# Grouped attention's front: a search round spread over gaps, keys and queries in a new order

## The reference

```python
# layer 1, feed-forward
xq = int4_quant(x); gate = square(relu(xq @ w_gate_q)); up = xq @ w_up_q      # 512 -> 1376
x = x + int8_quant(up * gate) @ w_down_q                                       # 1376 -> 512
# layer 2, grouped attention: 32 query heads of 128, 8 key/value heads, context of 512
q = rmsnorm(layernorm(x) @ q_proj); k = rmsnorm(ctx @ k_proj); v = ctx @ v_proj
x = x + softmax(q @ k.T * scale + mask) @ v @ o_proj
# layer 3, attention: which of the 512 context rows are among the 154 largest, feature by feature
_, topk_idx = top_k(moveaxis(channel_map, 1, 2), 154)
```

## Time and profile before

| | us |
|---|---|
| median of three runs (lowest, highest) | 877.66 (877.02, 878.44) |
| the profiled execution's own time | 877.61 |
| its span, first to last instruction | 875.9 |
| TensorE busy in the span | 782.7 (89%) |
| VectorE busy | 716.4 (82%) |
| ScalarE busy | 519.3 (59%) |
| GpSimd busy | 429.3 (49%) |

### The profile page before, as it was taken

One profiled execution on the slowest core, in us unless ns is written; L12 is line 12 of the kernel. 1 busy time (PEld: TensorE's weight loads), 2 busy tenths in 40 slices (PEclk: granted clock), 3 DMA queues, 4 the chain that ended last, 5 costly groups with the idle time before them and its releaser, 6 DMA issues. The chain is left out here.

```text
span 875.9 us, 16423 instructions
## 1 busy us (share of the span) xinstructions
PE 782.7 (89%) x5140; PEld 635.4 (73%) x5146; DVE 716.4 (82%) x1732; ACT 519.3 (59%) x1408; POOL 429.3 (49%) x380
## 2 busy tenths in 40 slices
PE   1976899858978999999999999999999999678878
PEld 0474676524767898898898898898898898565456
DVE  7878998958777887887887887887887887964975
ACT  6864898846347557557557557557557557321421
POOL 3237087805225845845845845845845845622110
PEclk9999999979979999999999999999999999789989
DMA  8253245562300310310310310310310320203001
GB/s 309 87 176 138 75 146 198 172 195 76 91 7 1 118 53 8 108 53 5 108 55 6 101 61 2 104 62 1 100 66 0 101 67 0 72 25 117 1 0 49
DMA packets 39114, 68.23 MB, mean 78 GB/s; under 512 B 5729, under 2 KB 18593, under 8 KB 38946
## 3 DMA queue, kind: packets, MB, share of 16 engines
q1 hardware_dynamic: 39074, 67.73, 23.6%
HBM read 62.38 MB, written 5.34 MB: 77 GB/s over the span
## 5 line engine op out<-in xcount | busy, mean ns | idle before, releaser
L2230 DVE TENSOR_SCALAR_CACHE_REDUCE xn<-ctxT,candidate 128x512 bf16<-128x512 f32 x248 | 174.4, 741 | 0.1
L1962 ACT ACTIVATE layer_attention_probs<-xnT,stats 128x512 f32<-128x512 f32 x128 | 93.9, 734 | 133.7 <-DVE stats L2070 133.7
L1746 PE MATMUL bank<-layer_attention_keysT,layer_attention_queriesT 128*128 128x512 f32 x384 | 124.9, 435 | 3.3 <-DVE layer_attention_queriesT L2063 3.3
L2082 DVE TENSOR_TENSOR layer_attention_probsT<-bank,layer_attention_probsT 128x512 fp32r<-128x512 f32 x128 | 88.1, 688 | 40.7 <-ACT layer_attention_probsT L1970 39.4
L1746 PEld LDWEIGHTS bank<-layer_attention_probsT,layer_attention_values 128*128 128x128 f32 x768 | 99.9, 191 | 19.2 <-issue 9.1
L1746 PE MATMUL bank<-layer_attention_probsT,layer_attention_values 128*128 128x256 f32 x768 | 103.5, 285 | 10.2 <-DVE layer_attention_probsT L2082 9.9
L1970 ACT CAST layer_attention_probsT<-bank 128x512 fp32r<-128x512 f32 x128 | 74.8, 584 | 52.0 <-PE bank L1821 52.0
L1746 PE MATMUL bank<-layer_attention_wo,layer_attention_headsT 128*128 128x512 f32 x384 | 102.2, 409 | 3.8 <-issue 3.0
L1693 POOL TENSOR_TENSOR layer_attention_mixed<-layer_attention_mixed,xnT 128x512 f32<-128x512 f32 x32 | 52.2, 1632 | 86.8 <-DMA xnT<-inverse_sums 85.4
L1746 PE MATMUL bank<-layer_attention_l_wq,layer_attention_xnT 128*128 128x512 f32 x384 | 93.6, 392 | 0.7 <-DVE layer_attention_xnT L2131 0.7
L1746 PEld LDWEIGHTS bank<-layer_attention_l_wkv,layer_context_parts 128*128 128x128 f32 x720 | 88.4, 188 | 2.8
(11 more groups left out here) (320 smaller groups left out, 1664.2 us busy)
## 6 DMA issues: line engine op xcount, KB each, us to landing
layer_attention_l_raw_qo<-in_wqT SPq DMA_DIRECT2D x9, 1024.0 KB, 5.1
xnT<-inverse_sums SPq DMA_DIRECT2D x16, 512.0 KB, 3.7
layer_attention_l_raw_qo<-in_woT SPq DMA_DIRECT2D x8, 1024.0 KB, 6.8
tw_raw<-in_w_gateT SPq DMA_DIRECT2D x8, 688.0 KB, 5.4
tw_raw<-in_w_upT SPq DMA_DIRECT2D x8, 688.0 KB, 4.2
tw_raw<-in_w_downT SPq DMA_DIRECT2D x6, 768.0 KB, 4.5
layer_attention_l_raw_kv<-in_wkvT SPq DMA_DIRECT2D x9, 512.0 KB, 4.9
ternary<-tw_rounded SPq DMA_DIRECT2D x8, 344.0 KB, 2.7
```

What stands on the lines that cost most here:

```text
L1746: last = pe.matmul(out, stationary[f][a], moving[f][b], start=f == 0 and x == 0, stop=f == count - 1 and x == 2)
L1962: a.activation(probs[:, u % 3, :], masked[:, u % 2, :], ACT.Exp, bias=negmax[:, u:u + 1], scale=-1.0, accum_out=sums[:, u:u + 1]).then_inc ...
L2082: v.tensor_tensor(probsT[:, 1, p % 2, :, columns], T[u % 2][:, :].rearrange("p (c q) -> p c q", c=CPB), probsT[:, 0, p % 2, :, columns], A ...
L2230: own(k.nc.vector.tensor_scalar(k.flags[:, r % 2], row_tile(k.ctxT, r), k.candidate[:, r:r + 1].bitcast(F32), 0.0, ALU.is_gt, ALU.add, acc ...
```

## The change

Three things are done.

1. The search round that stood as one block in the front is taken apart. Its first two counts go into the feed-forward, ahead of and behind the first `inner_chunk`. Counts three and four stay in the front, behind the keys' low part. The update comes behind the last low part of the queries. These four counts write their flags into the first row of `k.xnT`, which nothing else uses then; the maximum of unit 0 writes there next and now waits for them.
2. TensorE projects both query tiles of the first batch before it turns tiles 2 and 3 of x. The keys are turned between the halves of the second tile's projection. The scores of unit 0 are made before the turn of query tile 1.
3. VectorE makes the low part of x's tile 0 before the last update, and the norm of tile 3 is spread out. ScalarE copies query tile 0, turns out the keys, then copies query tile 1. GpSimd scales the keys before the last root of x's norm.

The same counts, products and copies are made as before; their places, the scratch tile of four counts and the waits that go with them are what differs.

```diff
@@ feed-forward, VectorE
+                bisection_count(k, own, 0, first_flags(k))
                 for c in range(NC):
                     inner_chunk(0, c)
+                    if c == 0:
+                        bisection_count(k, own, 1, first_flags(k))
@@ front, GpSimd
-                for t in range(TPB, TILES):
-                    tile_norm_gpsimd(k, n, t)
 ...
-                for c in TURNS:
-                    norm(start, own, c)
+                tile_norm_gpsimd(k, n, 2)
+                norm(start, own, KEYS)
+                tile_norm_gpsimd(k, n, 3)
+                norm(start, own, 0)
+                norm(start, own, 1)
@@ project_q, TensorE
                         pe.wait_ge(k.last_updated, t + 1)
+                        pe.wait_ge(S_["xnT_low"], t + 1)
@@ front, TensorE
-                pe.wait_ge(S_["xnT_low"], 1)
-                for half in range(2):
-                    project_q(start, 0, half)
+                project_q(start, 0, 0)
+                project_q(start, 0, 1)
+                project_q(start, 1, 0)
+                turn_rows(start, KEYS)
+                project_q(start, 1, 1)
                 turn_x(2)
                 turn_x(3)
-                for half in range(2):
-                    project_q(start, 1, half)
-                turn_rows(start, KEYS)
+                turn_rows(start, 0)
                 project_kv(after(start), 0, 0)
+                scores(start, 0)
                 pe.wait_ge(S_["xnT_low"], TILES)
-                turn_rows(start, 0)
                 turn_rows(start, 1)
-                scores(start, 0)
                 scores(start, 1)
@@ front, ScalarE
+                copy_q(start, 0)
+                a.wait_ge(S_["keyscale_ready"], 1)
+                rowsT_high(start, KEYS)
+                copy_q(start, 1)
+                rowsT_high(start, 0)
                 turned_high(2)
                 turned_high(3)
-                for t in range(TPB):
-                    copy_q(start, t)
-                a.wait_ge(S_["keyscale_ready"], 1)
-                for c in TURNS:
-                    rowsT_high(start, c)
+                rowsT_high(start, 1)
@@ front, VectorE
                 last_update(2)
                 tile_variance_vector(k, 2)
+                turned_low(0)
                 last_update(3)
-                turned_low(0)
-                tile_variance_vector(k, 3)
                 turned_low(1)
                 tile_rows_vector(k, n, 2)
-                tile_rows_vector(k, n, 3)
+                tile_variance_vector(k, 3)
 ...
                 values_low(start, 1)
+                tile_rows_vector(k, n, 3)
+                rowsT_low(start, KEYS)
+                for j in range(FRONT_COUNTS, 4):
+                    bisection_count(k, own, j, first_flags(k))
+                rowsT_low(start, 0)
                 turned_low(2)
                 turned_low(3)
-                for j in range(4):
-                    bisection_count(k, own, j)
+                own.wait()
+                maximum(start, 0)
+                rowsT_low(start, 1)
                 bisection_update(k, own)
-                for c in TURNS:
-                    rowsT_low(start, c)
-                maximum(start, 0)
@@ the search
+FRONT_COUNTS = 2
+def first_flags(k):
+    return k.xnT[:, 0, :].bitcast(BF16).rearrange("p (j c) -> p j c", j=2)
```

6 lines of the change are left out of this document (3 added, 3 removed).

## The result

The changed kernel takes 873.60 us (median of 14 runs, 870.46 to 877.89); the kernel before, run beside it, takes 877.67 (14 runs, 876.79 to 880.28). The ratio of the two is recorded as 0.9936, with a 95% interval of 0.9917 to 0.9955: 5.6 us less, between 3.9 and 7.3. The two medians themselves lie 4.1 us apart, so the gain is known to a microsecond or two and not to a tenth. The forecast was 7.2. Two later comparisons on other chips gave 0.9937 [0.9908, 0.9966] and 0.9922 [0.9887, 0.9956]; by the medians it is 5.8 us less in both. In the last of these, two of the 25 runs of before were slow ones (1014 and 2969 us); without them its median is 880.63, and the ratio counts neither.

What follows compares the result with a forecast made beforehand. TensorE bounds the steady steps, so the front's gain comes through whole: 5.4 us to unit 1's scores plus 1.8 for the clock make 7.2, from 877.61 to 870.4 us. Range 868.8 to 873.4.

Steps and rivals of the forecast that it cites:

- Feed-forward's counts at no cost: Feed-forward: two counts hide in VectorE's idle 0.58 and 2.42 us; cost nothing, 2.9 us if both covers failed.
- First projection 0.7 us earlier, keys' turn at 239.1: Front, TensorE: first query projection starts at 234.8, 0.7 us earlier; keys turned at 239.1 between halves of tile 1's projection.
- Counts hold query tile 0, scores of unit 0 at 244.8, of unit 1 at 248.0: Front: counts hold query tile 0's low part 0.6 us; unit 1's scores at 248.0 instead of 253.39, gaining 5.4.
- Clock, 1.8 us: Front at full clock: unit 1's scores to the turn of its probabilities (the mark) in 4.66 us instead of 6.43.
- the stretch at 276: Kernel before, 276 to 278 us: TensorE busy 0.87 of 2 us yet clock 1.00; cited against a clock fall.
- Sum 7.2: Whole kernel: 5.4 us up to unit 1's scores plus 1.8 for the clock, giving 870.4.
- through the steady steps whole: Attention's steady steps: TensorE busy 63.84 of 64 us, no slack, so the front's gain is neither lost nor caught up.
- the forecast's own sign for it: Wrong if the distance between the two profiles grows or shrinks by over 1 us between 255 and 745.
- slower rival: Tail running 7 us earlier has its low-clock stretches fall elsewhere; with 10 us of such work 880.4; chance 0.03.
- the clock rival: Clock falls in the new front too: from unit 0's scores 873.4, only behind unit 1's scores 872.2; chance 0.10.
- The rivals of the feed-forward, of VectorE and of the keys' turn: Feed-forward counts show: 871.3 to 873.3, 0.07; VectorE holds first units: 871.6, 0.07; keys' turn blocks second half-projection: 872.1, 0.03.

Runs made afterwards that it cites:

- search alone: Kernel before with two search counts moved into the feed-forward, two and the update where the whole round stood, TensorE's order unchanged: 876.66 us, ratio 0.9960.
- its fillers: Kernel before with 18 unread filler matmuls in TensorE's 4.29 us stop ahead of query tile 0's turn: 877.82 us, ratio 0.9981.
- order alone: Changed kernel with all four counts in the front behind the keys' low part, none in the feed-forward: 877.52 us, ratio 0.9988 to the kernel before.

## Why the prediction was right where it was, and what it missed

**Feed-forward's counts at no cost:** right. First product 194.51 (194.6 worked out), second at 196.89 with 0.30 us of idle time left of 2.42. The front starts 0.58 us earlier than before, not through the change: fronts start between 230.00 and 233.58 over all profiles. From the first gate product (190.49 in the earlier trace rows) to the front's start it is 41.3 us in the mean of the five profiles without the counts and 41.5 in that of the nine with them, each spread over more than 1 us, so no cost is shown.

**First projection 0.7 us earlier, keys' turn at 239.1:** right. 234.38 and 238.57, which is 2.73 and 6.92 after the front's start; worked out were 2.6 and 6.9. The load of the key scale cost 0.42 where 0.4 was the upper end, hidden as said.

**Counts hold query tile 0, scores of unit 0 at 244.8, of unit 1 at 248.0:** right. 244.28 and 247.53; from the front's start 12.63 and 15.88, worked out 12.6 and 15.8. The update ran from 247.30 on and hid behind the scores.

**Clock, 1.8 us:** right in the profiled pair, 4.65 us from those scores to the mark where 4.66 was worked out, and from there to the first load of inverse sums 22.13 us against 22.08 before, so the first units neither gave nor took. But the 6.43 us that it was taken from is the slowest of three draws: in the two other profiles of before's front the same way took 5.61 and 6.16, as the clock came back sooner, and against these the term is 1.0 and 1.5. And its reason was too simple. The forecast set it down to the absence of a long stop. The search alone shows a fall at stops of 1.72 and 1.40; the changed kernel shows full clock and half clock with the same stops. The Trainium skill's rule on swings of the clock ("TensorE: Matmul & The Clock Gate", "A second HAM failure mode: psum-queue depth-cycling"), which the forecast weighed against the stretch at 276, agrees with one profile of the five and not with four. The rival had 0.10, and one fall in five doesn't refute that. Its price was 1.6 us here (22.14 against 20.53), below the 1.8 and 3.0 that it was given for its two cases.

**Sum 7.2, of which 5.6 came** (4.1 by the medians). Up to the mark the profiled pair shows 7.64, and 7.06 without the front's start. The step that failed is "through the steady steps whole", and the forecast's own sign for it was met: it called itself wrong if the distance between the two profiles changed by over 1 us between 255 and 745, and this distance is 7.59 us at the first load of inverse sums and 3.45 fourteen steps later. The front's mechanism held, but the terms on both sides of that step were single draws.
- The front of before is drawn too. It took 27.59 us in the profile that the sum was made from, and 26.78 and 26.87 in two others with the same front; the mean is 27.08. The five of after have a mean of 20.79 with the one that fell. That is 6.3 us.
- The steady steps were said to have no slack to lose or gain. They have a term of 0 to 3 held updates at about 1.3 us each, and the profile of before drew none. But fronts as before drew 0, 2 and 3 (before, its fillers, search alone) and kernels with the front of after 3, 1, 2, 0 and 0 (the order alone: 3). These means, 1.7 and 1.2, don't differ in so few. So nothing shows that the change brings the 4.1 us that the profiled pair gave back here or that it removes them, and I take them for chance.
- The tail of the five kernels with the order of before lasts 97.4 us in the mean (96.60 to 98.49), that of the eight with the front of after 98.3 (96.27 to 100.48); the order alone had 96.23. If these 0.8 us are real, 6.3 - 0.8 = 5.5 is left. With the three and the five profiles that the 6.3 was taken from it is 97.2 against 98.6, and 4.9 is left. A spread of 2 to 4 us between profiles, and of 4.1 to 5.8 between the three differences of medians, lets neither be told from the 5.6, and where the rest of the 7.2 went stays open. The slower rival was of this kind, at 10 us, and is refuted at that size.

The stated range reached from 868.8 to 873.4. By the ratio the changed kernel stands at 872.0, inside it; its median of 873.60 is 0.2 above. The range reached down to a gain of 4.2 us for the clock rival's sake, and so it covered a shortfall that mostly had other reasons: that is luck in part. One slip of arithmetic: the chances of the faster cases make 0.97, and less 0.02 that is 0.95, not 0.94.

The rivals of the feed-forward, of VectorE and of the keys' turn did not occur.

## What to carry to other kernels

A front that waits can pay twice: in the stop, and in the clock behind it where that falls. Two edits that each shorten the stops may give less alone than together, if only both keep the clock up; one profile of each shows this here and the kernels' times don't, so it is a reason to try them together before one is dropped, and no more. And before a sum is made against one profile, look at which of its rows are draws: a stretch whose length depends on which of two engines comes first by 0.1 us belongs to the range, for before as well as for after.
